# A graph layer's neighbour maximum: count, selection, masks and late ranks moved to other uses, and a reordered start

## The reference

```python
h = jnp.maximum(_layernorm(x, axis=-1), 0.0)
mask = A != 0
pri = -jnp.arange(N, dtype=jnp.float32)
vals, idx = jax.lax.top_k(jnp.where(mask, pri, neg_inf), 25)
feats = jnp.where(valid[..., None], X[idx], neg_inf)   # valid = vals > neg_inf
agg = feats.max(axis=2)
agg = jnp.where((degree <= 25)[..., None], jnp.maximum(agg, 0.0), agg)
out = jax.nn.relu(jnp.einsum('bnf,fo->bno', concat([X, agg]), W) + b)
x + out
```

## Time and profile before

| what | value |
|---|---|
| median of 3 runs | 750.21 us (750.12 to 751.39) |
| the profiled execution's own time | 756.99 us |
| its span | 755.3 us |
| PE busy | 607.5 us (80%) |
| DVE busy | 612.1 us (81%) |
| ACT busy | 425.0 us (56%) |
| POOL busy | 49.6 us (7%) |
| mean granted TensorE clock | 0.966 |

### The profile page before, as it was taken

One profiled execution on the slowest core, in us unless ns is written; L12 is line 12 of the kernel. 1 busy time (PEld: TensorE's weight loads), 2 busy tenths in 40 slices (PEclk: granted clock), 3 DMA queues, 4 the chain that ended last, 5 costly groups with the idle time before them and its releaser, 6 DMA issues.

```text
span 755.3 us, 9644 instructions
## 1 busy us (share of the span) xinstructions
PE 607.5 (80%) x2689; PEld 243.3 (32%) x2720; DVE 612.1 (81%) x813; ACT 425.0 (56%) x579; POOL 49.6 (7%) x38
## 2 busy tenths in 40 slices
PE   0555499888989799888889798898888699897975
PEld 0111133333333333334333333343333333342322
DVE  6111398987989789897989788997989498998986
ACT  0366374866367482686568483767569373746210
POOL 3000000300003000110003000210002000210000
PEclk9997699999999999999999989999999899999999
DMA  9584443547544663538744563548544662230100
GB/s 302 191 250 158 122 162 85 213 124 245 161 167 146 144 248 77 187 140 236 214 160 151 136 249 90 192 144 269 167 174 146 200 220 54 88 122 29 56 15 14
DMA packets 107877, 117.94 MB, mean 156 GB/s; under 512 B 74435, under 2 KB 94150, under 8 KB 103366
## 3 DMA queue, kind: packets, MB, share of 16 engines
q1 hardware_dynamic: 107846, 117.61, 49.1%
HBM read 58.85 MB, written 20.97 MB: 106 GB/s over the span
## 4 chain that ended last, share of the span: by engine, by line
PE 34%; DVE 24%; issue 15%; ACT 11%; SPq 10%; DMA 5%; DVEq 1%; ACTq 0%; another core or an unknown queue 0%
PE picked L556 10%; DVE best L729 9%; PE picked L557 9%; DVE late_hot L735 5%; PE ring L505 4%; SPq L239 4%; ACT late_rank L401 3%; DVE hot L710 3%; PE side L517 3%; SPq L241 3%; PE side L516 3%; SPq L263 3%; DMA mask_t<-mask 3%; DVE best L828 3%; ACT late L413 2%
## 5 line engine op out<-in xcount | busy, mean ns | idle before, releaser
L729 DVE TENSOR_TENSOR best<-picked,best 128x1024 f32<-128x1024 f32 x224 | 268.2, 1217 | 43.4 <-PE picked L557 42.3
L556 PE MATMUL picked<-hot,h_hi 128*128 128x512 f16 x512 | 201.4, 393 | 42.4 <-DVE best L729 28.9
L557 PE MATMUL picked<-hot,h_lo 128*128 128x512 f16 x512 | 199.9, 390 | 0.0
L408 ACT ACTIVATE chosen<-side,bias_cut 128x512 bf16<-128x512 f32 x128 | 88.0, 687 | 117.5 <-PE side L517 107.0
L556 PE MATMUL picked<-late_hot,hi_skew 128*128 128x512 f16 x336 | 127.6, 380 | 12.5 <-DVE late_hot L735 8.5
L557 PE MATMUL picked<-late_hot,lo_skew 128*128 128x512 f16 x336 | 127.3, 379 | 0.0
L828 DVE TENSOR_TENSOR best<-picked,best 128x1024 f32<-128x1024 f32 x84 | 102.6, 1221 | 8.2 <-PE picked L557 8.2
L401 ACT ACTIVATE late_rank<-ring,late_bias 128x512 bf16<-128x512 f32 x128 | 81.7, 688 | 44.3 <-PE ring L505 40.9
L710 DVE TENSOR_SCALAR hot<-rank 128x4096 f16<-128x4096 bf16 x64 | 83.3, 1303 | 26.7 <-ACT rank L401 26.7
L556 PEld LDWEIGHTS picked<-hot,h_hi 128*128 128x128 f16 x512 | 50.9, 99 | 153.5 <-DVE best L729 73.5
L437 ACT COPY best<-picked 128x1024 f32<-128x1024 f32 x32 | 32.3, 1014 | 113.5 <-PE picked L557 113.5
(11 more groups left out here) (72 smaller groups left out, 381.2 us busy)
## 6 DMA issues: line engine op xcount, KB each, us to landing
adj_in<-in_adj_dram SPq DMA_DIRECT2D x15, 2048.0 KB, 7.9
kept<-chosen SPq DMA_DIRECT2D x128, 128.0 KB, 1.8
picks<-kept SPq DMA_DIRECT2D x16, 1024.0 KB, 4.7
late_skew<-late SPq DMA_DIRECT2D x32, 192.0 KB, 2.3
x_in<-in_x_dram SPq DMA_DIRECT2D x8, 512.0 KB, 8.5
xres<-in_x_dram SPq DMA_DIRECT2D x16, 256.0 KB, 7.8
late_skew<-late SPq DMA_DIRECT2D x16, 256.0 KB, 2.4
late_skew<-late SPq DMA_DIRECT2D x32, 128.0 KB, 2.1
```

The lines of the kernel that those rows point to most:

```text
L408: nc.scalar.activation(chosen[:, k, :], side[:, :], ACT.Sign, bias=bias_cut[:, 0:1], scale=-1.0).then_inc(chosen_made, 1)
L556: nc.tensor.matmul(dst, hi[:, slot, k, :], onehot, start=start, stop=False)
L557: return nc.tensor.matmul(dst, lo[:, slot, k, :], onehot, start=False, stop=stop)
L729: nc.vector.tensor_tensor(best[:, half, s, :, :], picked[s][:, :, :], best[:, half, s, :, :], ALU.max).then_inc(picked_read, 1)
```

## The change

It moves pieces to other uses and reorders the prologue; the loop has the same compute instructions as before.

- Selection links stand at uses 6 to 13 (before 4 to 11), rank pieces at uses 5 to 11 (before 4 to 11).
- Of the 8 late rank pieces, 6 stay at the end of the step and the last two stand after use 4 of the next step. `count_rounds` on DVE stands after `take_pair` of use 4 of the group itself (before: ahead of it, at the end of the step before).
- The four masks stand at uses 5, 8, 10 and 12 (before: together, after the uses). `find_late` stands after all uses (before: two at use 12, two at use 14).
- The statistics of the next batch stand in the even step, uses 13 to 15 (before: odd step, uses 4 to 6), the gain in the odd step at use 5 (before use 8).
- SP loads adjacency g+4 at the start of step g (before at its end), and `xres` two groups ahead.
- Prologue: the four adjacency quarters are loaded ahead of `x`, the adjacency of group 1 is loaded behind the first transposes, the first group's choices are read back in two halves of 64 partitions, and two of the late rank pieces leave it.

```diff
-    SELECT_WITH, RANK_WITH = spread_over(4, 11), spread_over(4, 11)
-
-    FLAG_USES, RELU_USE, LATE_HOT_USES = (12, 14), 13, (7, 9)
-    STATS_USES, MOMENTS_USE, SPREAD_USE, GAIN_USE = (4, 5), 6, 7, 8
+    SELECT_WITH, RANK_WITH = spread_over(6, 13), spread_over(5, 11)
+    LATE_EARLY, LATE_REST_USE, COUNT_USE, LATE_HOT_USES = 6, 4, 4, (7, 9)
+    MASK_USES, RELU_USE = (5, 8, 10, 12), 13
+    STATS_USES, MOMENTS_USE, GAIN_USE = (13, 14), 15, 5
...
@@ SP @@
+            def first_picks(i):
+
+                part = slice(i * (P // 2), (i + 1) * (P // 2))
+                sp.wait_ge(first_stored[i], 16 * HALF)
+                sp.dma_start(picks[part, :, :], kept_by_class[part]).then_inc(first_loaded, 16)
...
-            load_x(0)
             for q in range(Q):
                 sp.dma_start(adj_in[:, 0, q * N:(q + 1) * N], adj_v[0][:, q * N:(q + 1) * N]).then_inc(adj_first[q], 16)
-            load_adj(1, 1)
+            load_x(0)
...
                 sp.dma_start_transpose(mask_t[:, :, q * P:(q + 1) * P], mask[:, q, :]).then_inc(mask_turned, 16)
+            load_adj(1, 1)
             load_adj(2, 0)
-            store_chosen(True)
-            load_picks(None)
+            sp.reg_add(chosen_due, chosen_due, K)
+            for k in range(K):
+                sp.wait_ge(chosen_made, k + 1)
+                sp.dma_start(kept_by_block[k], chosen[:, k, :]).then_inc(first_stored[k // HALF], 16)
+                if k == K - 2:
+                    first_picks(0)
+            first_picks(1)
...
@@ ACT @@
                 for use in range(PAIRS, USES):
+                    if use == LATE_REST_USE:
+                        for k in range(LATE_EARLY, K):
+                            stage(at + REST_AT, k, late_rank, late_bias[:, k:k + 1])
+                    for k in RANK_WITH[use] if more else []:
+                        stage(at + RANK_AT, k, rank[:, (u + 1) % 2], late_bias[:, 0:1])
                     for k in SELECT_WITH[use] if not at_end(it, u, 2) else []:
                         choose(g + 2, k)
-                    for k in RANK_WITH[use] if more else []:
-                        stage(at + RANK_AT, k, rank[:, (u + 1) % 2], late_bias[:, 0:1])
-                    if use == SPREAD_USE and new_batch:
-                        spreads(batch)
+                    if use in MASK_USES and not at_end(it, u, 3):
+                        make_masks((u + 1) % 2, [MASK_USES.index(use)])
                     if use == RELU_USE and new_batch:
                         relu_parts(batch, slot)
-                    if use in FLAG_USES and more:
-                        for p in range(2):
-                            p += 2 * FLAG_USES.index(use)
-                            find_late(p, (u + 1) % 2, at + RANK_AT + 2 * p + 2)
+                if more:
+                    for p in range(PAIRS):
+                        find_late(p, (u + 1) % 2, at + RANK_AT + 2 * p + 2)
                 if new_batch:
                     turned_h(batch, slot)
-                if not at_end(it, u, 3):
-                    make_masks((u + 1) % 2)
...
@@ PE @@
                     pick_pair(g, use, slot)
+                    if use == LATE_REST_USE:
+                        for k in range(LATE_EARLY, K):
+                            late_ranks(g, at + REST_AT, k)
+                    for k in RANK_WITH[use] if more else []:
+                        ranks(g + 1, at + RANK_AT, k)
                     for k in SELECT_WITH[use] if not at_end(it, u, 2) else []:
                         place(g + 2, k, (CHAINS + 1) * g + 1)
-                    for k in RANK_WITH[use] if more else []:
-                        ranks(g + 1, at + RANK_AT, k)
...
@@ DVE @@
                     take_pair(g, use, s)
                     if use == 5:
                         make_hot(BASE, s)
+                    if use == COUNT_USE:
+                        count_rounds(g, s)
...
```

More of the change, by code:

```diff
@@ L169, in build @@
         picks_loaded = sem("picks_loaded")
+        first_stored = [sem(f"first_stored{i}") for i in range(2)]
+        first_loaded = sem("first_loaded")
         ring_read = sem("ring_read")
@@ L296, in _ @@
             load_xres(0, 0)
+            load_xres(1, 1)
             sp.reg_add(masks_due, masks_due, Q)
@@ L393, in make_masks @@
                 act.wait_ge(adj_loaded[slot], adj_due[slot])
-                for q in range(Q):
+            def make_masks(slot, quarters):
+                if 0 in quarters:
+                    await_masks(slot)
+                for q in quarters:
                     counts = adj_in[:, slot, q * N:(q + 1) * N].bitcast(U32)
@@ L403, in choose @@
             def choose(g, k):
-                if k == 0 and not (isinstance(g, int) and g == 0):
-                    act.wait_ge(chosen_stored, LANDED * g)
+                if k == 0 and isinstance(g, int) and g == 1:
+                    for i in range(2):
+                        act.wait_ge(first_stored[i], 16 * HALF)
+                elif k == 0 and not (isinstance(g, int) and g == 0):
+                    act.wait_ge(chosen_stored, LANDED * (g - 1))
                 act.wait_ge(place_written, g * K + k + 1)
@@ L445, in _ @@
                 choose(0, k)
-            make_masks(1)
+            make_masks(1, range(Q))
             turned_h(0, 0)
@@ L449, in _ @@
             for k in range(K):
-                stage(RANK_AT, k, rank[:, 0], late_bias[:, 0:1])
+                stage(0, k, rank[:, 0], late_bias[:, 0:1])
             find_late(0, 0, K)
@@ L457, in _ @@
                 choose(1, k)
-            for k in range(K):
-                stage(LATE_AT, k, late_rank, late_bias[:, k:k + 1])
-            make_masks(0)
+            for k in range(LATE_EARLY):
+                stage(K, k, late_rank, late_bias[:, k:k + 1])
+            make_masks(0, range(Q))
             def step(it, u):
@@ L607, in _ @@
                 place(1, k, None)
-            for k in range(K):
-                late_ranks(0, LATE_AT, k)
+            for k in range(LATE_EARLY):
+                late_ranks(0, K, k)
             pe.wait_ge(chosen_made, 2 * K)
@@ L660, in step @@
                     late_ranks(g + 1, at + LATE_AT, 2)
+                    pick_pair(g + 1, 3, next_slot)
                     late_ranks(g + 1, at + LATE_AT, 3)
-                    pick_pair(g + 1, 3, next_slot)
                 project(g, it, u, new_batch)
                 if more:
-                    for k in range(HALF, K):
+                    for k in range(4, LATE_EARLY):
                         late_ranks(g + 1, at + LATE_AT, k)
@@ L749, in _ @@
                 nc.vector.memset(held[:, i:i + 1], 0.0).then_inc(opened, 1)
+            for q in range(Q):
+                first_mask(q)
             stats_of(0, range(K))
             moments_of(0)
-            first_mask(0)
             make_gain(0)
-            for q in range(1, Q):
-                first_mask(q)
             dve.wait_ge(basics_made, 11)
@@ L800, in step @@
                 batch = batch_of(it, u + 1)
+                ahead = u % PER_BATCH == 0 and not at_end(it, u, PER_BATCH)
                 for use in range(PAIRS, USES):
@@ L806, in step @@
                         make_hot(BASE, s)
+                    if use == COUNT_USE:
+                        count_rounds(g, s)
                     if use in LATE_HOT_USES:
-                        dve.wait_ge(ring_read, at)
+                        dve.wait_ge(ring_read, at + REST_AT + K)
                         make_late_hot(LATE_HOT_USES.index(use), numbers[:, 1:2])
-                    if use in STATS_USES and new_batch:
+                    if use in STATS_USES and ahead:
                         half = STATS_USES.index(use)
-                        stats_of(batch, range(half * HALF, (half + 1) * HALF))
-                    if use == MOMENTS_USE and new_batch:
-                        moments_of(batch)
+                        stats_of(batch_of(it, u) + 1, range(half * HALF, (half + 1) * HALF))
+                    if use == MOMENTS_USE and ahead:
+                        moments_of(batch_of(it, u) + 1)
                     if use == GAIN_USE and new_batch:
```

37 lines of the change are left out of this document (21 added, 16 removed).

## The result

| | before | changed |
|---|---|---|
| median of 4 runs each | 750.80 us (750.12 to 754.99) | 767.09 us (764.80 to 768.18) |
| the profiled execution's own time | 756.99 us | 764.80 us |
| its span | 755.3 us | 762.9 us |
| mean granted TensorE clock | 0.966 | 0.968 |

The ratio is 1.0201 [1.0157, 1.0246]: the changed kernel is slower, by 1.6 to 2.5%. The direction was as forecast. The size was not: 750.2 to 756.5 is +0.8%, and the time lies just above the upper end of the range (766). The two profiled executions differ by only 7.8 us, against a forecast of 6.4 between them, while the medians lie 16.3 apart. The profiled execution of before (756.99) is longer than all four of its timed runs, that of the change is the shortest of its own.

The account below looks back on a forecast made before the run. PE and DVE, each about 80% busy, bound the kernel by handing pairs through two PSUM tiles. Gains (-23.0 tails, -7.0 prologue) and losses summed to +6.4 on 757.0, scaled 756.5; range 738 to 766, rivals included.

Parts of the forecast that it names:

- The masks on SP: SP's chain from late to transposed masks: masks land 7.1 into step 2, PE waits 3.2 (before 2.6), so the wait stays.
- The tails: Last late maximum to next first pair: three late rank matmuls move behind use 4, each 1.5 shorter, -23.0 in all.
- The odd uses: First pair to first late maximum, odd steps 1 to 11: 23.8 against 23.0, masks stalling the selection chain by 1.9; +5.1.
- in an odd step 0.3 for the gain and 1.5 for POOL come on top: DVE's own work in an odd step's uses: 20.1 plus these two make 21.9.
- The even uses: First pair to first late maximum, even steps 2 to 12: late masks make them 25.9, +15.6; clock falls add +10.8.
- so I add four falls at 2.7: Clock falls behind the mask waits in even steps: +10.8, between 0 and 16.2.
- the 4.2: DVE's loss to late pairs in each of the even steps 2 to 12, which start with the wait for masks.
- The prologue: Start before step 0: first place near 18 instead of 21.98 (-4.0), picks -1.6, fewer late pieces -1.4; together -7.0.
- A second half by itself might take 3.5, -1.6: Prologue's reading back of picks, 5.09 from last store to landing before: gain between 0 and -2.
- Two late pieces fewer: 2 x 0.7: Two late rank pieces leave the prologue: -1.4.
- Step 0: Uses of the first step: selection begins later and statistics come on top, 32.4 before, about 33.9 now, +1.5.
- The rival on the other side: ACT stalls do not come and the clock holds: -10.4, about 740; chance 0.34 with all cases below 748.7.

Follow-up runs that it names:

- a_swap: The changed kernel with SP transposing the masks ahead of the 14 feature shift DMAs in odd steps: 751.66 us, ratio to before 0.9999.
- a_masks_end: The changed kernel with the four masks put back behind the uses, all else as changed: 750.27 us, ratio to before 0.9997.
- c_both: The changed kernel with the edits of a_swap and a_masks_end together: 741.01 us, ratio to before 0.9823.
- c_gain: c_both with the gain at use 9 instead of use 5: 730.00 us, ratio to before 0.9666.
- c_sel: c_both with selection links and rank pieces back at uses 4 to 11: 731.44 us in three runs, ratio to before 0.9675.
- b_swap: The kernel before with SP transposing the masks ahead of the 14 feature shift DMAs in odd steps: 739.24 us, ratio 0.9849.
- b_nohalves: The kernel before with the new start, but the first choices read back in one load instead of two halves: 744.83 us in one run.

## Why the prediction came out as it did

*The masks on SP: right, shown.* For step 2 the forecast held to 0.1 us (7.2 into the step, wait 3.16); in the other even steps PE waited 0.48 to 2.65, and in step 8 not at all. a_swap takes the lateness away and a_masks_end takes ACT out from behind it while PE still waits; each brings the changed kernel back to the time before, and c_both goes 26 below. The prediction's statement that masks in time would be worth 15 or more came out at 15.4.

*The tails: right, undersized.* I counted the three matmuls behind the projection (1.55 measured against 1.53). The tail is 1.9 shorter. The remaining 0.35 lies further ahead, where two late pieces fewer pass between PE and ACT; I did not test it. Step 11's tail, forecast 3.2 longer by its shifts and 1.5 shorter by the count, became 2.2 longer.

*The odd uses: wrong in size, and the term was incomplete.* "Odd uses: 21.9 + 1.9 = 23.8" was 25.05. The masks in the chain cost 0.7 (a_masks_end) instead of 1.9. The failed step is "in an odd step 0.3 for the gain and 1.5 for POOL come on top": I took POOL's interference over from before, but the change moves both of POOL's appointments. The gain at use 5 puts POOL's second pass on `late_hot`, 1.57 in each odd step (11.0 in seven; before 5.1), and the features put `h_lo` on `hot` for 1.8 (12.4 in seven; before 5.5). Together the 1.5 became 3.35. With the measured sizes the sum is 20.1 + 0.3 + 3.35 + 0.7 = 24.45; the 0.6 up to 25.05 stays open. The masks were 1.2 too high and POOL 1.85 too low, so the forecast looked closer than its terms were. c_gain shows the first part of POOL's (24.33 to 22.54), c_sel fits the second. The DVE rows of before had the hint: `hot` at 2.00 against 1.22. The question that I did not ask is where that POOL pass would stand after the change. The Trainium skill, "SBUF — State Buffer", section "SBUF: two separate sides", says that a GpSimd instruction and certain VectorE instructions take a shared port pair for their whole length, and whichever comes second waits entirely. The trace agrees: both ends fit POOL's end plus the undisturbed duration to within 0.2, `late_hot` took its 0.74 in c_gain and `hot` its 1.22 in c_sel once POOL was elsewhere, while the maxima that read `picked` ran undisturbed beside POOL (2.36 for two at 129.92).

*The even uses: path right, the clock oversized.* Written out without a fall, an even step was to take 26.2, or 25.9 with the value taken; step 10, the one without a fall, took 25.70. The failed step is "so I add four falls at 2.7": +10.8. Falls came in five of six steps, at 0.93 or 0.94, and the pair of steps 6 and 10 prices one at 1.2; five of these are 6.0 (an estimate). I had read 2 to 4 for a fall from the even steps of before. But its steps 4 and 8 also hold an idle of ACT of about 5, and step 12 a wait of 5.46, so these are not the price of the clock. Six times 25.9 and 6.0 are 161.4, measured 161.6. That this is so close is luck in part, since steps 4 and 8 hold ACT's idle here too. The other 2.1 of the 6.7 is the starting point: I had 23.3 for an even step before, and the mean was 23.65. By the Trainium skill, "TensorE: Matmul & The Clock Gate", section "What's actually happening", all six would fall. The trace agrees in five; step 10 kept 1.00 behind the same wait of 2.65 as step 6. All this is from one pair of profiles of nearly equal clock. In the timed runs the changed kernel's clock is lower by 0.009, so the clock's part was larger there.

*Also in the 4.2:* I read all of an even step's loss as the masks'. b_swap shows that steps 4 and 8 hold an idle of 4 to 5 on ACT that has nothing to do with them. The changed kernel has it too, at rank pieces: 1.87 in step 4, 2.72 and 2.84 in step 8. It spoilt the price of a fall, and it made me expect too much of the cure.

*The prologue: wrong by 5.* The first `place` came at 18.3 (forecast 18), 3.7 earlier, so that part held. "A second half by itself might take 3.5, -1.6" failed: the halves cost 1.3 to 1.5 (b_nohalves, and 8.3 against 6.8 in the profiles). The rule quoted from the Trainium skill, "DMA: Bandwidth & Descriptors", section "Rules for kernel authors", was right, and even optimistic for this case, since besides bringing nothing the first half delays the last store. "Two late pieces fewer: 2 x 0.7" was 0.5: from the last link to the first pair it takes 5.78, before 6.30. Another 0.7 lies in the prologue's second selection chain, 12.07 against 11.40. Its links take 1.38 at first and 1.81 later in both kernels, and the 1.81 begins earlier now; from 60 to 74 us the granted clock is 0.50, before 0.63.

*Step 0: wrong in sign.* "About 33.9 now" was 31.12. The masks landed 11.0 into the uses (forecast 11.3). From 87 to 106 us the granted clock was 0.95, before 0.83; whether that is the cause was not tested.

*The rival on the other side* (ACT's stalls do not come, about 740) failed at its own point of decision: PE's `place` for `chosen` went from 16 waits to 37, and its weight load's wait from 35.7 to 66.9 us.

*The sum.* +6.4 against +7.8 between the profiles looks better than it is. The prologue, the odd uses and steps 13 to 15 were too low by 4.9, 7.3 and 3.0 (the count in step 15 was forgotten, and step 13 has POOL's part); the even uses, the tails and step 0 too high by 6.7, 4.3 and 2.8. Errors of both signs cancelled, which was luck. To the median of 767 the remainder is that the profile of before was longer than its timed runs; I scaled 757.0 down by 0.9%, and the changed kernel's runs did not scale with it. Their clock is lower than before's, as the section on the result has it.

## What to carry to other kernels

When a change moves work on GpSimd or the VectorE instructions around it, lay the two timelines over each other again as they will stand after the move; a collision of 1.5 a step became 3.35, and one number in a table took half of it away. When a wait ends with a transfer, ask when its issue chain begins and what stands on that queue ahead of it: making the masks earlier brought nothing, reordering the queue brought 12 to 15. Before adding a penalty such as a clock fall, take its price from two steps with the same waits: here 1.2 from such a pair, where steps that also held another idle had suggested 2.7. When two profiles are compared, put the mean clock of the timed runs beside them.

## What was not expected of the hardware

- GpSimd's float32 passes of 1.90 held float16 `late_hot` (0.74 to 2.31), and its `h_lo` of 2.13 held `hot` (1.22 to 3.02), but the float32 maxima that read the PSUM tiles `picked` took 1.18 each beside it.
- In the kernel before and in b_swap, ACT stood 4.4 to 5.2 us with no wait to be seen at the first step of the second and third loop iteration. Written out as straight code the idle went, but the program's time did not change (726.47 against 726.35, 751.43 against 751.99).
- With a read of 64 partitions issued ahead of it on the same queue, the last store of the choices landed in 3.44 instead of 1.70.
- PE's wait for late masks sums to less in the changed kernel (11.1 against 16.3 in steps 2 to 12), and the mean clock of the steps with a fall is higher (0.93 to 0.94, before 0.86 to 0.93). In step 4 of the changed kernel the clock fell with a wait for masks of 0.48, in step 8 with none; what decides a fall was not found.
